# bf16 parts from PSUM in one fused VectorE instruction, their cast on ScalarE, and the first group's stacks loaded in two halves

## The reference, cut to what matters

```python
q = jnp.einsum('btc,hcd->bhtd', xn, Wq) + bq[None, :, None, :]
k = jnp.einsum('bsc,hcd->bhsd', kv_src, Wk) + bk[None, :, None, :]
...
scores = jnp.einsum('bhtd,bhsd->bhts', q, k) / scale    # scale = DH ** -0.5
...
xn1 = _ln(x, g1, be1)
sa = _mha(xn1, xn1, ..., causal=True)
x = x + (sa @ W1 + b1)
xn2 = _ln(x, g2, be2)
ca = _mha(xn2, encoder_out, ..., causal=False)
x = x + (ca @ W2 + b2)
xn3 = _ln(x, g3, be3)
ff = jax.nn.relu(xn3 @ Wf1 + bf1) @ Wf2 + bf2
return x + ff
```

## Time and profile before

| | before |
|---|---|
| time, median of 3 runs (lowest, highest) | 626.71 us (624.55, 627.41) |
| span of the profiled execution, from its first to its last instruction | 631.5 us |
| busy PE, DVE, ACT, POOL in it | 504.7, 368.2, 307.5, 187.8 us |
| mean granted TensorE clock | 0.884 of full speed |

### The profile page before, as it was taken

One profiled execution on the slowest core, in us unless ns is written; L12 is line 12 of the kernel. 1 busy time (PEld: TensorE's weight loads), 2 busy tenths in 40 slices (PEclk: granted clock), 3 DMA queues, 4 the chain that ended last, 5 costly groups with the idle time before them and its releaser, 6 DMA issues.

```text
span 631.5 us, 8807 instructions
## 1 busy us (share of the span) xinstructions
PE 504.7 (80%) x3296; PEld 296.2 (47%) x3296; DVE 368.2 (58%) x695; ACT 307.5 (49%) x590; POOL 187.8 (30%) x276
## 2 busy tenths in 40 slices
PE   1775775999997999799988835669576757989887
PEld 0664452344443444344333333434222446988877
DVE  4887697678886788678532147645221763454430
ACT  3544020667765776477666502247443535253460
POOL 3788821131221132122132523305131350121200
PEclk9988697799999999899999969767555968999998
DMA  8138936007367335727260266978333212101001
GB/s 288 47 109 158 201 116 118 0 21 116 52 120 105 67 66 107 115 56 38 83 186 1 68 168 92 173 108 140 107 99 115 81 47 72 34 0 34 18 17 34
DMA packets 41930, 56.51 MB, mean 89 GB/s; under 512 B 12832, under 2 KB 27424, under 8 KB 41888
## 3 DMA queue, kind: packets, MB, share of 16 engines
q1 hardware_dynamic: 39584, 47.56, 38.1%
q10 hardware_dynamic: 2304, 8.39, 3.8%
HBM read 35.12 MB, written 20.42 MB: 88 GB/s over the span
## 4 chain that ended last, share of the span: by engine, by line
PE 44%; DMA 23%; DVE 15%; ACT 6%; SPq 5%; issue 3%; POOL 2%; ACTq 0%; DVEq 0%
PE ps L864 10%; PE ps L973 9%; PE ps L948 8%; PE ps L911 7%; DMA arena_h<-heads 6%; DMA stacks<-shift_t 6%; PE ps L1060 5%; DMA recips<-recip_rows 4%; DVE max_a L1141 4%; ACT arena_p L732 4%; DMA heads<-out_t 4%; DVE xn L1094 3%; SPq L409 2%; PE ps L933 2%; SPq L428 2%
## 5 line engine op out<-in xcount | busy, mean ns | idle before, releaser
L732 ACT ACTIVATE arena_p<-ps 128x512 f32<-128x512 f32 (+4 forms) x416 | 190.9, 541 | 129.5 <-PE ps L948 127.3
L1141 DVE TENSOR_REDUCE max_a<-ps 128x1 f32<-128x512 f32 (+4 forms) x280 | 159.6, 620 | 46.6 <-PE ps L911 34.0
L948 PE MATMUL ps<-stacks 99*128 99x512 bf16 (+2 forms) x448 | 149.9, 369 | 27.6 <-DMA stacks<-shift_t 22.5
L911 PE MATMUL ps<-stacks 96*128 96x77 bf16 (+4 forms) x640 | 146.2, 306 | 32.1 <-DVE max_a L1141 19.1
L911 PEld LDWEIGHTS ps<-stacks 96*128 96x128 bf16 x640 | 58.9, 111 | 97.5 <-DVE max_a L1141 45.5
L973 PE MATMUL ps<-arena_p,v_group 128*32 128x512 f32 (+4 forms) x896 | 94.1, 540 | 0.7 <-POOL arena_p L617 0.5
L617 POOL TENSOR_SCALAR_AFFINE_SELECT arena_p<-arena_p 128x512 f32<-128x512 f32 x64 | 41.0, 653 | 169.9 <-ACT arena_p L732 169.9
L948 PEld LDWEIGHTS ps<-stacks 99*128 99x128 bf16 (+1 forms) x448 | 45.6, 107 | 93.1 <-ACT arena_p L732 37.8
L1141 DVE TENSOR_REDUCE max_b<-ps 128x1 f32<-128x384 f32 (+3 forms) x88 | 52.5, 636 | 21.3 <-PE ps L915 21.3
L864 PE MATMUL ps<-wf2r,hid_r 128*128 128x256 f32 x384 | 49.9, 294 | 9.6 <-DVE hid_r L1254 9.6
L864 PEld LDWEIGHTS ps<-wf2r,hid_r 128*128 128x128 f32 x384 | 49.1, 202 | 10.7 <-DVE hid_r L1254 10.7
(11 more groups left out here) (68 smaller groups left out, 528.1 us busy)
## 6 DMA issues: line engine op xcount, KB each, us to landing
heads<-out_t ACTq DMA_DIRECT2D x16, 512.0 KB, 4.3
stacks<-q_parts SPq DMA_DIRECT2D x48, 128.0 KB, 5.2
stacks<-k_parts SPq DMA_DIRECT2D x48, 128.0 KB, 7.6
stacks<-qc_parts SPq DMA_DIRECT2D x48, 128.0 KB, 5.1
arena_h<-heads SPq DMA_DIRECT2D x8, 512.0 KB
recips<-recip_rows SPq DMA_DIRECT2D x8, 512.0 KB
q_parts<-parts SPq DMA_DIRECT2D x8, 384.0 KB, 2.5
k_parts<-parts SPq DMA_DIRECT2D x8, 384.0 KB, 2.6
```

The costliest lines, as they stand in the source:

```text
L732: nc.scalar.activation(probs[0:a.kp, a.probs_slot(g, ui), h, k * BANK:k * BANK + width], ps[0:a.kp, unit % S_BANKS, 0:width], ACT.Exp, sca ...
L911: ins = nc.tensor.matmul(m_bank(use)[:, o:o + w], q_stack[0:ROWS, g % a.nb, h, t * P:(t + 1) * P], k_rows(ROWS, g, h, s0, s0 + w), start=T ...
L948: ins = nc.tensor.matmul(ps[0:keys, unit % S_BANKS, lo - k * BANK:hi - k * BANK], k_rows(ROWS_S, g, h, i * P, i * P + keys), q_stack[:, g ...
L1141: nc.vector.tensor_reduce(dst, m_bank(use)[:, 0:nh * w].rearrange("p (h w) -> p h w", h=nh), AX.X, ALU.max).then_inc(s.max_read, 1)
```

## The change

For a unit, ACT now writes only the first part from PSUM. DVE makes the remainder in one `scalar_tensor_tensor` that reads PSUM, adds the bias column and subtracts the first part; ACT casts the remainder to the second part, one unit behind (`second_part` of u stands after `first_part` of u + 1). `full` is gone as a buffer of its own and `rest` has four buffers. A PSUM bank of a unit is now free when DVE has read it (`split_v`), where it was free when ACT had read it (`split_a`). The units of a row chunk come in the order q, k, q, k: units 0 and 1 are then q and k of output channels 0 to 127. Group 0's stacks are loaded in two halves of 512 rows, 12 DMAs each: the first behind the store of unit 3, the second behind unit 7. Chunks 0 to 10 of group 0 move into the middle of qkv(2), behind its second unit; chunks 11 to 13 stay behind qkv(2) and wait for the second half.

```diff
@@ SP
+            def load_half(half):
+                lo, hi = half * CHUNK, (half + 1) * CHUNK
+                arrived = S1.q_in[0] if half else half_in
+                for slot in range(2):
+                    sp.wait_ge(parts_out[slot], parts_landed(4 * half + slot))
+                load_blocks(q_dram, q_stack[:, 0, :, :], QP, slice(0, 1), arrived, lo, hi)
+                load_blocks(k_dram, k_self[:, 0, :, :], KP, slice(0, 1), arrived, lo, hi)
             for u in range(U_QC):
-                if u == 2 * NCH:
+                if u in (NCH, 2 * NCH):
+                    load_half(u // NCH - 1)
+                if u == 3 * NCH:
                     wait_parts(2 * NCH)
-                    load_stacks(SELF, S1, 0)
-                if u == 3 * NCH:
                     load_stacks(SELF, S1, 1)
                 store_parts(u)
@@ ACT
-                at_least(act, split_v, 2 * (u - 2) + 1)
-                nc.scalar.activation(full[:, u % 2, 0:width], src, ACT.Identity, bias=col[:, c:c + 1])\
-                    .then_inc(split_a, 1)
+            def second_part(u):
+                width, _, _ = split_unit(u)
+                act.wait_ge(split_v, u + 1)
+                nc.scalar.activation(parts[:, u % 4, 1, 0:width], rest[:, u % 4, 0:width], ACT.Copy)\
+                    .then_inc(split_b, 1)
+            def split(units):
+                first_part(units[0])
+                for u, after in zip(units, units[1:]):
+                    first_part(after)
+                    second_part(u)
+                second_part(units[-1])
@@ PE
                     elif c == 3 or c == 0 and n:
-                        pe.wait_ge(split_a, 2 * (u - 3 if c else u - 1) + 2)
+                        pe.wait_ge(split_v, (u - 3 if c else u - 1) + 1)
...
+                    if n == NCH - 2 and s == 1:
+                        attention(SELF, S1, 0, SELF.late_chunk)
@@ DVE
-                dve.wait_ge(split_a, 2 * u + 2)
-                at_least(dve, split_p, u - 1)
-                nc.vector.tensor_tensor(r, f, p[:, 0, :], ALU.subtract).then_inc(split_v, 1)
-                dve.wait_ge(split_v, 2 * u + 1)
-                nc.vector.tensor_copy(p[:, 1, :], r).then_inc(split_v, 1)
+                dve.wait_ge(split_a, u + 1)
+                at_least(dve, split_p, u - 3)
+                nc.vector.scalar_tensor_tensor(rest[:, u % 4, 0:width], ps[:, unit_bank(u), 0:width],
+                                               col[:, c:c + 1], parts[:, u % 4, 0, 0:width], ALU.add, ALU.subtract)\
+                    .then_inc(split_v, 1)
...
             for n in range(3):
+                if n == 2:
+                    attention(SELF, S1, 0, SELF.late_chunk)
                 for u in range(4):
                     split(4 * n + u)
                 add_v(n)
```

More of the change, by code:

```diff
@@ L96, in __init__ @@
                 self.chunks += [(t, h, nh, s, w) for h in range(0, GH, nh)]
+        self.late_chunk = [c[0] >= CT for c in self.chunks].index(True) if causal else 0
         if causal:
@@ L289, in build @@
         xn_t = scratch(2, KC, CHUNK)
-        full = scratch(2, CHUNK)
-        rest = scratch(2, CHUNK)
+        rest = scratch(4, CHUNK)
+        full = rest[:, 0:2, :]
         ps = ctx.enter_context(nc.psum_tensor("ps", [P, 8, 512], F32))
@@ L314, in build @@
         acc_full, acc_read = sem("acc_full"), sem("acc_read")
-        split_a, split_v, split_p = sem("split_a"), sem("split_v"), sem("split_p")
+        split_a, split_v, split_b, split_p = (sem(n) for n in ("split_a", "split_v", "split_b", "split_p"))
+        half_in = sem("half_in")
         parts_out = [sem(f"parts_out{s}") for s in range(4)]
@@ L768, in _ @@
                 if k:
[L769 to L774, removed]
+                    split(range(4 * (k - 1), 4 * k))
+            split(range(4 * (NCH - 1), U_QC))
             act.wait_ge(split_p, U_QC)
@@ L784, in _ @@
                     copy_norm(NCH + n)
-                for u in range(2):
-                    split(U_QC + 2 * n + u)
+                split(range(U_QC + 2 * n, U_QC + 2 * n + 2))
             act.wait_ge(split_p, U_H)
@@ L903, in chunk @@
                     t, h0, nh, s0, w = a.chunks[c]
-                    if c == 0:
+                    if c == 0 and g == 0 and a.causal:
+                        pe.wait_ge(half_in, 16 * len(QP) * 2)
+                    elif c == (a.late_chunk if g == 0 else 0):
                         pe.wait_ge(s.q_in[g % a.nb], 16 * len(QP) * (1 + a.causal) * (g // a.nb + 1))
@@ L994, in _ @@
                     qkv(k - 1)
-            attention(SELF, S1, 0, SELF_EARLY[0])
+            attention(SELF, S1, SELF.late_chunk, SELF_EARLY[0])
             qkv(NCH - 1)
@@ L1097, in split @@
             def split(u):
-                width, _, _ = split_unit(u)
-                p, f = parts[:, u % 4, :, 0:width], full[:, u % 2, 0:width]
-                r = rest[:, u % 2, 0:width]
-                dve.wait_ge(split_a, 2 * u + 2)
-                at_least(dve, split_p, u - 1)
-                nc.vector.tensor_tensor(r, f, p[:, 0, :], ALU.subtract).then_inc(split_v, 1)
-                dve.wait_ge(split_v, 2 * u + 1)
-                nc.vector.tensor_copy(p[:, 1, :], r).then_inc(split_v, 1)
+                width, c, _ = split_unit(u)
+                dve.wait_ge(split_a, u + 1)
[3 more added lines that the diff above has]
+                    .then_inc(split_v, 1)
             def add_v(n):
```

38 lines of the change are left out of this document (19 added, 19 removed).

## The result

The changed kernel took 619.96 us (median of 4 runs, 618.9 to 621.49) against 627.06 us (median of 4 runs, 624.55 to 630.32) for the kernel before in the same comparison: a ratio of 0.9857, 95% interval 0.9814 to 0.9901. By the ratio it is faster by about 9 us, 6 to 12 by the interval; the two medians by themselves lie 7.1 us apart; 10.0 was forecast. The unaltered changed kernel in a later comparison gave 0.9833 (0.978 to 0.9886), about 10.5 us.

The account below looks back on a forecast made before the run. The prediction took the chain of waits to the self-attention's score 0 (111.5 us) as the bound. Score 0 9.3 us earlier plus 0.75 in the cross-attention made 10.0: 626.71 to 616.7 us, range 613.5 to 622.5.

Parts of the forecast that it names:

- my own case: Whole kernel: the forecast gain of 10.0 us, time 614 to 619.5 us; chance 0.74.
- the rival in which POOL holds the fused instruction: DVE's fused instruction takes 1.48 us beside POOL, costing 5.6 us together: 622.3 us; band 619.5 to 622.5, chance 0.13.
- LayerNorm of row chunk 3 ends: On DVE, ahead of unit 4's fused instruction: from 42.07 us before to 41, between 42.1 and 39.6.
- unit 4's fused instruction to chunk 0: DVE and PE before chunk 0: at full clock chunk 0 at 50.7 us, with 1.5 lost to the clock 52.2.
- The half loads: Group 0's stacks: each half takes 7.1 to 14.1 us; first lands 42.3 to 49.3, second 57.2 to 64.2.
- The memset: POOL's 10.33 us memset behind unit 11's third part: covered by some 2 us; a much larger gain would end here.
- DVE loses four casts, 1.4 us: From chunk 11 to the context's first unit, four casts at 0.34 us each leave DVE: 1.4 us.
- The first half was not late: Rival: first half lands behind 52.2 us, PE and DVE stand still; time 617 to 627; chance 0.04.
- The clock did not stay low: Rival: PE stays at 1.2 GHz from unit 7 to score 0; about 643 us; chance 0.04.
- The sign that I named for it: PE: a granted clock of 0.5 beyond 60 us would show the forecast wrong.
- More than 13 us: Rival of more gain: no clock lost (1.5), LayerNorm at 39.6 (1.4), 12.9 us, time 614; chance 0.05.
- The cross-attention: Sixth query unit: without the float32 copy ahead, third parts end about 393.6 us; loads and shift 0.75 us earlier.

Follow-up runs that it names:

- the early fused instructions: The changed kernel with the fused instructions of units 4 to 6 ahead of the apply of row chunk 3's LayerNorm on DVE: 612.01 us, ratio 0.9755.
- the halves alone: The kernel before with the unit order q, k, q, k, the half loads and the early chunks, keeping its old subtraction and cast: 628.79 us, ratio 1.0055.
- POOL's work woven between the pieces: The kernel before with half loads, early chunks, a twelve-piece memset, and POOL's third parts of units 12 to 14 between pieces: 622.75 us, ratio 0.99.
- the pieces in a row: The kernel before with half loads and early chunks, and POOL's memset cut into twelve at the same place: 626.95 us, ratio 0.9998.
- unit 15's second part ahead: The changed kernel with unit 15's second part ahead of unit 16's first part on ACT: 618.93 us, ratio 0.9804.
- both edits: The changed kernel with units 4 to 6's fused instructions before LayerNorm's apply and unit 15's second part before unit 16's first: 613.36 us, ratio 0.9695.

## Why the prediction was right, point by point

The mechanism held: score 0 is what moved, and what stands behind it moved by no more than two executions of one kernel differ. The size is less sure. The gain is 9.0 us by the ratio and 7.1 by the medians, for 10.0, and the median of 619.96 us lies in the whole range (613.5 to 622.5) but half a microsecond above my own case (614 to 619.5), in the band that I gave to the rival in which POOL holds the fused instruction. That it is not that rival is shown by the trace and not by the time. The terms, from the trace of the changed kernel:

| step of the prediction | forecast | measured |
|---|---|---|
| fused instruction | 0.69 (0.68 to 1.48) | 0.74 to 0.75, two in a row 1.40 |
| ACT's second part | 0.65 | 0.62 to 0.63 |
| first half landed | 42.3 to 49.3 | about 40.2 |
| LayerNorm of row chunk 3 ends | 41 (39.6 to 42.1) | 39.72 |
| PE's wait before unit 7 | some 4 | 4.72 |
| unit 4's fused instruction to chunk 0 | 10.5, of it 1.5 for the clock | 10.1, of it 2.1 for the clock |
| chunk 0 | 52.2 | 50.51 |
| chunk 11 read | 65.6 | 63.26 |
| from there to ACT's first context unit | 18.7 | 18.56 |
| context to group 2's loads | 4.7 | 4.92 |
| loads to score 0 | 13.3 | 13.72 |
| score 0 earlier by | 9.3 | 11.1 |

The clock's 2.1 is (2.92 - 1.65) + (3.69 - 2.87): the chain's two rows against their full-clock lengths in the same chain, 1.65 for six matmuls of a unit and 2.87 for 24 of the v rows.

**The sizes that were off.** Three terms together make score 0 earlier than forecast. LayerNorm ended at the early one of my two bounds (1.3 us earlier than taken). POOL's four third parts take 4.58 us in a row, near the four times 1.17 that I had, but they also begin 1.4 us earlier (26.91; before, 28.29) and so end 3.7 us earlier, not 2.2 to 2.9. Of these 3.7 us LayerNorm kept 2.35; POOL's low halves, which now wait 1.25 us for ACT's copies, took most of the rest, the part that I had left without a number. From the fused instruction to chunk 0 I added whole durations of rows that overlap one another, 1.0 us too much; the clock, 0.6 dearer than taken, took back part of it. From chunk 0 to the end of the reading of chunks 0 to 10 it took 6.80 us (50.51 to 57.31) and not 7.35, since before it had begun with PE at half clock behind the load. Against them stand 0.2 and 0.4 us in the last two stretches before score 0.

**The half loads.** I bounded the landing by the bytes: half the bytes, 7.1 to 14.1 us. In fact SP's issuing sets it. SP's timeline:

```profile
31.99 3.11 SPq L412 DMA_DIRECT2D stacks<-q_parts  x6
35.15 2.77 SPq L412 DMA_DIRECT2D stacks<-k_parts  x6
```

Twelve issues take 5.9 us, and a DMA of these lands 2.3 us behind its issue (the median of the trace's list of DMA issues): 8.2 us, near the lower bound. They also begin 3.2 us earlier than the 35.2 of the forecast, since the third parts end earlier. Nothing hung on it, as the prediction said; PE came 10 us later.

**The memset.** The prediction said that a gain much larger than 10 would end at the memset, with 2 us of cover. That was wrong in its premise: I held the memset at its forecast place while varying the gain, but it follows unit 11's third part and moves forward with it. With the early fused instructions the memset began 6.4 us earlier (59.68 for 66.10), and score 0 came a further 5.2 us forward without meeting it. Nor did the prediction see what the memset really threatens, DVE's casts. The fused split removes these casts, so it did not matter here; the step "DVE loses four casts, 1.4 us" named the small part of what their going is worth beside early chunks.

**The rivals.** The fused instruction is not held by POOL: 0.74 to 0.75 us beside third parts and beside the memset. The first half was not late. The clock did not stay low: the granted clock was 1.00 in 46 to 48 and stayed there until 88. The sign that I named for it, 0.5 beyond 60 us, was too wide: the clock reads 0.50 over 90 to 106, around PE's wait for the shift, as it did around the same wait in the kernel before (104 to 116). The Trainium skill's "TensorE: Matmul & The Clock Gate", section "HAM oscillation — how this bites in real kernels", says that groups of matmuls with waits between them each start cold. The trace agrees: unit 7 took 2.92 us for 1.65, and the v rows 3.69 for 2.87. That every group up to chunk 0 would stay cold, which gave 59.7, was my own addition; the trace has chunk 0 at 50.51. More than 13 us did not come: the trace's 12.0 for both places is inside my case (7.2 to 12.7 us), near its upper end, and the times give less.

**The cross-attention.** For its sixth unit, from the first part's start to the end of the second of two third parts it is now 3.60 us, 375.65 to 379.25 in the chain; before, 3.88 to the third part's end. With the float32 copy gone ahead of it (some 0.6 in the forecast's working, not measured apart), that is 0.9; forecast 0.75. How much of it reaches the scores is not shown: the shift's DMA there took 9.01 us in this execution and 8.15 before.

The interval of the ratio leaves 6.2 to 11.7 us. The forecast of 10.0 is in it; the 12.0 that the trace of one execution gives for the two places (11.1 + 0.9) lies at its upper edge.

## What to carry to other kernels

Where two edits are made at once, ask for each what it brings forward into the other's neighbourhood: here the early chunks alone made the kernel slower, since they moved a SBUF-to-SBUF cast in front of the end of a long GpSimd instruction, and the fused split, which reads PSUM, took that obstacle away. With POOL's work woven between the pieces the early chunks paid even without the fused split. Write a long GpSimd instruction in pieces, with the work that others wait for between them, or put it where VectorE only reads PSUM. When a PSUM bank is freed later than before, look at what the new reader is queued behind: moving three short instructions ahead of a LayerNorm gave 4.9 to 6.4 us, half to two thirds as much again as the whole change. And before two executions are compared at a point behind a DMA, look at how long that DMA took in each: here it moved score 0 by up to 2 us, with no edit to that DMA.

## What the runs showed of the hardware

- A VectorE cast from SBUF to SBUF that meets a GpSimd memset waits for the end of that one instruction, at both lengths tried: 8.50 us beside a memset of 10.33, 0.83 to 0.90 beside pieces of 0.94 (11.32 us for twelve), 0.43 alone. A subtraction with both inputs in SBUF was not held by the memset (0.68 us at 69.68 and 70.26), but was by third parts, which read SBUF (1.55 at 81.51).
- The Trainium skill, "SBUF — State Buffer", section "Who interferes with whom", says this: a cast can run in a mode that takes the port pair which VectorE shares with GpSimd, and of the two engines the one that comes second is then blocked for the other's whole instruction; an instruction with two SBUF inputs contends with a GpSimd instruction that reads SBUF and not with one that only writes it; and one with at most one SBUF input, outside those modes, does not contend with GpSimd. The rows here agree with all three, the fused instruction (one input in PSUM, one in SBUF, and a column; 0.74 to 0.75 us everywhere) being the last.
- A wait of 4.1 to 4.7 us cost PE about the same clock whichever group of matmuls stood behind it: 2.1 us with unit 7 first, 2.3 with the v rows first. Filling the wait with unit 7 saved unit 7, not the clock; removing the wait saved both.
- The clock of one stretch can differ between executions. At the end of chunks 0 to 10, whose matmuls wait for DVE's reductions, the granted clock fell to 0.50 for 2 to 3 us in four executions with the early chunks (the halves alone, the pieces in a row, unit 15's second part ahead, both edits) and stayed at 1.00 in the other six. In the two of them that have the fused split chunk 11 then came about 0.7 us later.
- The shift's DMA took 5.36 to 7.85 us from execution to execution, 6.29 and 5.36 in two of the same kernel.
